# Batch statistics inside the fourth pass and a last stage in lots of four tiles

## The reference

```python
    out = D_inv[:, None] * jax.ops.segment_sum(e_feat[col], row, num_segments=num_nodes)
    out = out + b
    mean = out.mean(axis=0)
    var = out.var(axis=0)
    out = gamma * (out - mean) * jax.lax.rsqrt(var + BN_EPS) + beta
    return jax.nn.relu(out)
    ...
    x = x + _L3_gnn_ref(h, edge_index, L3_gnn_hyperedge_weight, L3_gnn_W, L3_gnn_b, L3_gnn_gamma, L3_gnn_beta)
```

## Time and profile before

| | us |
|---|---|
| median of 3 runs (lowest to highest) | 2605.35 (2597.77 to 2607.53) |
| the profiled execution's own time | 2608.04 |
| its span, first to last instruction | 2606.2 |
| TensorE busy, share of the span | 2320.7, 89% |
| VectorE busy | 1603.8, 62% |
| ScalarE busy | 1230.0, 47% |
| mean granted clock of TensorE | 0.952 |

### The profile page before, as it was taken

One profiled execution on the slowest core, in us unless ns is written; L12 is line 12 of the kernel. 1 busy time (PEld: TensorE's weight loads), 2 busy tenths in 40 slices (PEclk: granted clock), 3 DMA queues, 4 the chain that ended last, 5 costly groups with the idle time before them and its releaser, 6 DMA issues. The chain is left out here.

```text
span 2606.2 us, 71305 instructions
## 1 busy us (share of the span) xinstructions
PE 2320.7 (89%) x27901; PEld 1993.0 (76%) x27901; DVE 1603.8 (62%) x3678; ACT 1230.0 (47%) x2680; POOL 44.6 (2%) x51
## 2 busy tenths in 40 slices
PE   2489999999989998999929999899998999999996
PEld 1368778878777887887828888788887888888884
DVE  6689999999999998999962333334433112121224
ACT  2478878878777786877731222222232000011113
POOL 3300000000000000000000000000000000000000
PEclk8589999999999998999969999999998999999996
DMA  6479999999999999999989999899998999999994
GB/s 191 106 157 201 216 214 208 210 218 209 212 181 220 212 212 175 222 199 212 218 211 251 283 285 283 223 260 258 258 259 208 290 288 290 263 246 248 266 270 110
DMA packets 1608879, 589.27 MB, mean 226 GB/s; under 512 B 964326, under 2 KB 1605354, under 8 KB 1608471
## 3 DMA queue, kind: packets, MB, share of 16 engines
q1 hardware_dynamic: 1604773, 579.88, 99.9%
q0 software_dynamic: 1600, 4.92, 0.7%
q10 hardware_dynamic: 2226, 0.62, 0.2%
HBM read 255.26 MB, written 89.20 MB: 132 GB/s over the span
## 5 line engine op out<-in xcount | busy, mean ns | idle before, releaser
L1174 ACT CAST stage<-ps 128x784 f16<-128x784 f32 x784 | 655.4, 836 | 106.0 <-DMA counts_by_source<-stage 69.7
L649 PE MATMUL ps<-Ha,a_tiles 128*128 128x258 f16 x4802 | 548.5, 274 | 46.6 <-ACT Ha L1221 39.2
L649 PEld LDWEIGHTS ps<-Ha,a_tiles 128*128 128x128 f16 x4802 | 470.1, 98 | 117.1 <-ACT Ha L1221 39.3
L602 PE MATMUL ps<-hot_c,hot_r 128*128 128x98 f16 x3136 | 509.5, 212 | 13.6 <-DVE hot_c L885 7.4
L603 PE MATMUL ps<-hot_c,hot_r 128*128 128x98 f16 x3136 | 503.5, 211 | 0.0
L604 PE MATMUL ps<-hot_c,hot_r 128*128 128x98 f16 x3136 | 501.7, 210 | 0.0
L1159 ACT CAST stage<-ps 128x392 f16<-128x392 f32 x784 | 397.9, 508 | 142.5 <-PE ps L585 142.5
L577 PE MATMUL ps<-g_in,wt 128*128 128x128 f16 x2401 | 431.0, 222 | 35.9 <-DVE X L897 17.3
L578 PE MATMUL ps<-g_in,wt 128*128 128x128 f16 x2401 | 429.3, 222 | 0.0
L579 PE MATMUL ps<-g_in,wt 128*128 128x128 f16 x2401 | 429.2, 222 | 0.0
L897 DVE SCALAR_TENSOR_TENSOR X<-ps,X 128x512 f32<-128x512 f32 (+1 forms) x637 | 392.4, 650 | 49.4 <-PE ps L579 49.3
(11 more groups left out here) (194 smaller groups left out, 2062.1 us busy)
## 6 DMA issues: line engine op xcount, KB each, us to landing
a_tiles<-counts_by_source SPq DMA_DIRECT2D x147, 1600.0 KB, 8.8
counts_by_source<-stage SPq DMA_DIRECT2D x49, 1600.0 KB, 8.0
gated_parts<-G SPq DMA_DIRECT2D x7, 448.0 KB, 3.6
g_in<-gated_parts SPq DMA_DIRECT2D x98, 32.0 KB, 3.1
out_x<-X SPq DMA_DIRECT2D x6, 512.0 KB
edge_table<-tab SPq DMA_DIRECT2D x1, 2448.0 KB, 10.5
wt<-stage SPq DMA_TRANSPOSE x98, 10.9
dst_run<-in_dst SPq DMA_DIRECT2D x1, 612.4 KB
```

Source lines behind the costliest of these rows:

```text
L602: mm(into(0), rows_, codes(0), start=v == 0, stop=True, skip_group_check=True)
L649: last = mm(ps[:, c % 2, 0:PARTS], a_slot(ph, c, i), moving[:, i], start=i == 0, stop=i == TILES - 1)
L1174: a.copy(stage[:, b, 0:2, 0:TILES, u * SET_COLS:(u + 1) * SET_COLS], of).then_inc(s("hi_done"), 1)
```

## The change

- In pass four, in odd steps from j = 5, VectorE takes the statistics of a pair of tiles of `OT` (256 columns), behind its sum of tile j. It waits for the block of tile j-4 (`upd_done4` at j-3). In the loop, `OT` and `stats` are addressed by a register. Behind the branch two statistics are left (columns 5888 to 6144 and 6144 to 6250), and 25 are joined in place of 13.
- The last stage goes in 13 lots of four tiles (`lot_tiles`; the last lot has one tile), all as written-out code. ScalarE normalises 512 columns in one instruction into one of three buffers of `ybig`, which lies where `hbig` of pass one was. TensorE turns four blocks into one bank, with banks 4 to 7 in turn, and signals once. VectorE adds 512 columns in one instruction.
- SyncE sends each lot on its own: twelve transfers of 256 KB and the one of 53 KB.

```diff
+def lot_tiles(n):
+
+    return slice(4 * n, min(4 * n + 4, TILES))
...
+        ybig, _ = at("ybig", [P, 3, 4, P], F32, o2 - 2 * SET * P * 4)
...
-            for g in range(6):
-                sp.wait_ge(s("x_out"), 8 * (g + 1))
-                sp.dma_start(out[g * 8 * P:(g + 1) * 8 * P].rearrange("(i p) f -> p i f", p=P), X[:, g * 8:(g + 1) * 8, :]).then_inc(s("out_stored"), 16)
-            sp.wait_ge(s("x_out"), TILES)
+            for n in range(FOURS - 1):
+                sp.wait_ge(s("x_out"), n + 1)
+                sp.dma_start(out[n * 4 * P:(n + 1) * 4 * P].rearrange("(i p) f -> p i f", p=P), X[:, lot_tiles(n), :]).then_inc(s("out_stored"), 16)
+            sp.wait_ge(s("x_out"), FOURS)
...
-                if on(j):
-                    pe.wait_ge(s("y_ready"), j + 1)
-                    if later(j, 2):
-                        pe.wait_ge(s("x_out"), j - 1)
-                    tr(ps[:, 4 + c % 2, 0:P], hrow[:, c % SLOTS], ident[:]).then_inc(s("y_turned"), 1)
+            for n in range(FOURS):
+                pe.wait_ge(s("y_ready"), n + 1)
+                if n >= 4:
+                    pe.wait_ge(s("x_out"), n - 3)
+                tiles = lot_tiles(n)
+                for i in range(tiles.stop - tiles.start):
+                    last = tr(ps[:, 4 + n % 4, i * P:(i + 1) * P], ybig[:, n % 3, i], ident[:])
+                last.then_inc(s("y_turned"), 1)
...
+                        if ph == 4 and c % 2 and later(j, 5):
+                            n = k * (SLOTS // 2) + (c - 5) // 2
+                            dve.wait_ge(s("upd_done4"), j - 3)
+                            pair = OT[:, 2 * n:2 * n + 2] if isinstance(n, int) else OT[:, bass.ds(n * 2, 2)]
+                            v.bn_stats(row(stats, n), pair.rearrange("p i n -> p (i n)"))
...
-            lots = [(a, min(a + 512, NODES)) for a in range(0, NODES, 512)]
-            for n, (a, z) in enumerate(lots):
-                last = v.bn_stats(stats[:, n], flat[:, a:z])
+            for n in (GROUPS - 2, GROUPS - 1):
+                last = v.bn_stats(stats[:, n], flat[:, 2 * n * P:min(2 * (n + 1) * P, NODES)])
...
-            c2(v.bn_aggr(fin[:, 0:2], stats[:, 0:len(lots)].rearrange("p n s -> p (n s)")))
+            c2(v.bn_aggr(fin[:, 0:2], stats[:, 0:GROUPS].rearrange("p n s -> p (n s)")))
...
-                if on(j):
-                    dve.wait_ge(s("y_turned"), j + 1)
-                    v.tensor_tensor(row(X, j), row(X, j), ps[:, 4 + c % 2, 0:P], ALU.add).then_inc(s("x_out"), 1)
+            for n in range(FOURS):
+                dve.wait_ge(s("y_turned"), n + 1)
+                tiles = lot_tiles(n)
+                xs = X[:, tiles].rearrange("p i f -> p (i f)")
+                v.tensor_tensor(xs, xs, ps[:, 4 + n % 4, 0:(tiles.stop - tiles.start) * P], ALU.add).then_inc(s("x_out"), 1)
...
-                if on(j):
-                    if later(j, SLOTS):
-                        act.wait_ge(s("y_turned"), j - (SLOTS - 1))
-                    a.activation(hrow[:, c % SLOTS], row(OT, j), ACT.Relu, bias=fin[:, 7:8], scale=fin[:, 5:6]).then_inc(s("y_ready"), 1)
+            for n in range(FOURS):
+                if n >= 3:
+                    act.wait_ge(s("y_turned"), n - 2)
+                tiles = lot_tiles(n)
+                y = ybig[:, n % 3, 0:tiles.stop - tiles.start].rearrange("p i n -> p (i n)")
+                a.activation(y, OT[:, tiles].rearrange("p i n -> p (i n)"), ACT.Relu, bias=fin[:, 7:8], scale=fin[:, 5:6]).then_inc(s("y_ready"), 1)
```

More of the change, by code:

```diff
@@ L448, in _ @@
             branch(sp, layers)
-            for g in range(6):
-                sp.wait_ge(s("x_out"), 8 * (g + 1))
-                sp.dma_start(out[g * 8 * P:(g + 1) * 8 * P].rearrange("(i p) f -> p i f", p=P), X[:, g * 8:(g + 1) * 8, :]).then_inc(s("out_stored"), 16)
-            sp.wait_ge(s("x_out"), TILES)
+            for n in range(FOURS - 1):
+                sp.wait_ge(s("x_out"), n + 1)
+                sp.dma_start(out[n * 4 * P:(n + 1) * 4 * P].rearrange("(i p) f -> p i f", p=P), X[:, lot_tiles(n), :]).then_inc(s("out_stored"), 16)
+            sp.wait_ge(s("x_out"), FOURS)
             sp.dma_start(out[(TILES - 1) * P:NODES], X[0:LAST, TILES - 1, :]).then_inc(s("out_stored"), 16)
-            sp.wait_ge(s("out_stored"), 16 * 7)
+            sp.wait_ge(s("out_stored"), 16 * FOURS)
         @block.gpsimd
@@ L683, in _ @@
             branch(pe, layers)
-            def last_step(j, k, c):
-                if on(j):
-                    pe.wait_ge(s("y_ready"), j + 1)
-                    if later(j, 2):
-                        pe.wait_ge(s("x_out"), j - 1)
-                    tr(ps[:, 4 + c % 2, 0:P], hrow[:, c % SLOTS], ident[:]).then_inc(s("y_turned"), 1)
-            tiles_loop(pe, last_step, 0)
+            for n in range(FOURS):
[6 more added lines that the diff above has]
+                last.then_inc(s("y_turned"), 1)
         @block.vector
@@ L1099, in _ @@
             v.tensor_tensor(fin[:, 7:8], cols[:, 3:4], fin[:, 6:7], ALU.subtract).then_inc(s("batch"), 1)
-            def last_step(j, k, c):
-                if on(j):
-                    dve.wait_ge(s("y_turned"), j + 1)
-                    v.tensor_tensor(row(X, j), row(X, j), ps[:, 4 + c % 2, 0:P], ALU.add).then_inc(s("x_out"), 1)
-            tiles_loop(dve, last_step, 0)
+            for n in range(FOURS):
[3 more added lines that the diff above has]
+                v.tensor_tensor(xs, xs, ps[:, 4 + n % 4, 0:(tiles.stop - tiles.start) * P], ALU.add).then_inc(s("x_out"), 1)
         @block.scalar
@@ L1263, in _ @@
             act.wait_ge(s("batch"), 1)
-            def last_step(j, k, c):
-                if on(j):
-                    if later(j, SLOTS):
-                        act.wait_ge(s("y_turned"), j - (SLOTS - 1))
-                    a.activation(hrow[:, c % SLOTS], row(OT, j), ACT.Relu, bias=fin[:, 7:8], scale=fin[:, 5:6]).then_inc(s("y_ready"), 1)
-            tiles_loop(act, last_step, 0)
+            for n in range(FOURS):
[4 more added lines that the diff above has]
+                a.activation(y, OT[:, tiles].rearrange("p i n -> p (i n)"), ACT.Relu, bias=fin[:, 7:8], scale=fin[:, 5:6]).then_inc(s("y_ready"), 1)
 _INS = ["x", "src", "dst", "edge_weight", "L0_gnn_W", "L0_gnn_W_gate", "L0_gnn_b_gate", "L1_gnn_W", "L1_gnn_b",
```

## The result

The changed kernel takes 2590.25 us (median of 7 runs, 2584.78 to 2594.58), beside 2606.26 for the one before (7 runs, 2597.77 to 2610.79). The ratio is 0.9933, 95% interval 0.9918 to 0.9948: faster by 0.7%, which is 17 us (the two medians lie 16.0 us apart). The forecast was 19.6 us less, 2585.7.

What follows compares the result with a forecast made beforehand. TensorE bounds nearly all the kernel, relay latency its end. Gains of 6.1 us ahead of the relay and 13.5 in it make 19.6, off the 2605.35 median: 2585.7 us, range 2578 to 2597.5.

Steps and rivals of the forecast that it cites:

- VectorE's restart: Behind the branch: 2.71 us before statistics start, possibly counted from VectorE's last operation, now a pair's statistic; +0.35 us.
- statistics at the end: Behind the fourth pass: 13 statistics of 7.39 us become two of 0.58 us together, a gain of 6.8 us.
- pause ahead of the aggregate: Between the last statistic and the aggregate on VectorE: the prediction gave no added wait here, 0 us.
- aggregate: Joining the statistics at the end: it reads 150 numbers in place of 78, a loss of 0.33 us (0 to 0.5).
- relay, first activation to the end: Last stage, ScalarE to TensorE to VectorE to output: lots of four replace single tiles, 13.5 us less.
- fourth pass: Pair statistics there were costed at nothing: VectorE is idle 4.8 us per tile, a pair's statistic takes about 0.41.
- Part 2: The last stage in 13 lots with four banks and three buffers: latency replaced by bandwidth, 13.5 us less.
- four paces: Last stage, per lot: ScalarE 0.73 us, TensorE 0.86, VectorE 0.68, transfer 0.904; the slowest, the transfer, sets the pace.
- The 2.37 us behind the last large burst: End of the span: the last 53 KB transfer stays as it is, 2.37 us, mostly at 44 GB/s.
- rival C: Behind the branch: code loading comes out of cover and delays ScalarE or TensorE, losing 1 to 2.7 us; 14%.
- TensorE's clock: Last stage: clock stays at 0.50, 1.2 GHz, so four transposes take 0.86 us per lot.
- the 2 that the prediction named: Sign of being right, at the end: the adds finish some 2 us ahead of the last bytes.

Runs made afterwards that it cites:

- half_stored: The changed kernel storing only two of the four tiles of each lot; 21.07 us from VectorE's last sum to the end, against 23.99.
- four_banks: The kernel before with four PSUM banks in turn in place of two, still one tile per instruction; ratio 0.9975 to the kernel before.
- lots_only: The changed kernel with all 13 statistics back at the end and none in the fourth pass, lots kept; ratio 0.9944 to the kernel before.
- pairs_thrice: The changed kernel taking each pair's statistics three times in the fourth pass; 22.37 us from VectorE's last sum to the end, against 23.99.
- pad_split: The changed kernel with 64 never-run VectorE instructions shifting the code and the last transfer sent as 96 and 10 rows; ratio 0.9918 to the kernel before.

## Why the prediction was right, and where it was not

The direction, the size (17 us by the ratio, 18.3 in the end part, against 19.6) and the mechanism of both parts hold. One wait was missed. Term by term, in us:

| term | predicted | measured |
|---|---|---|
| VectorE's restart | +0.35 | -0.03 (2.71 to 2.68) |
| statistics at the end | -6.81 | -6.79 (7.39 to 0.60) |
| pause ahead of the aggregate | 0 | +1.72 (0.04 to 1.76) |
| aggregate | +0.33 | +0.32 (0.51 to 0.83) |
| relay, first activation to the end | -13.5 | -13.5 (30.4 to 16.9) |
| fourth pass | 0 | +0.5 (last sum at 2564.41, not 2563.91), within the spread |
| sum, change of the span | -19.6 | -17.8 (2606.2 to 2588.4) |

- **Part 2 came out to a tenth of a microsecond.** Measured, with the forecast in brackets: activations 0.81 (0.80), adds 0.69 (0.68), a lot every 0.85 (0.86) for the first six, first lot done 2.71 us after its activation starts (2.79), 11 us of output without a pause (10.85). The step that carried it was to compare four paces and take the transfer; half_stored shows that it is the bound, four_banks that latency was it before. The 2.37 us behind the last large burst should have been 2.34 by the prediction's own figures (2606.2 - 2603.86), which changes nothing.
- **The step that failed is the way from the branch to the aggregate.** I counted one wait for code, the 2.71 us, and put its danger on the other engines: rival C had ScalarE late because the long statistics no longer cover it. ScalarE wasn't late: its root starts 0.04 us behind VectorE's operation ahead of it. (C's reckoning was off too: 2.71 us from the end of ScalarE's last operation, 2565.54, is 2568.25 and not 2567.9, still in time.) VectorE itself waited a second time, 1.76 us ahead of the aggregate, which the prediction had at nothing. That these lie in C's 1 to 2.7 is luck, since engine and reason were others. What the view could have told: in the earlier trace rows code packets still arrive after VectorE's restart at 2566.62, though nothing in the trace says whose they are.
- **The restart** was sized by the wrong rule. The 1.07 us behind OT didn't follow pair 22. Eleven of the twelve kernels that leave the branch first restart 2.64 to 2.85 us after the sum, with no statistic behind it (lots_only 2.85, four_banks 2.64), one (2.68) or three (pairs_thrice 2.76), and pad_split at 3.03. So the delay doesn't wait for VectorE's queued work to end; at what point it starts stays open.
- **TensorE's clock** was assumed to stay at 1.2 GHz. It rose to 2.4 GHz at 2578.4, after 6.0 us in which the transposes left no gap; in the relay before, busy for 13.9 of 19 us, it had stayed low. From then on the adds came every 0.60 us. The sum didn't need it, since the output was the bound at either clock: the adds ended at 2582.5, and the last bytes of the lots left at about 2586.3, 3.8 us behind and not the 2 that the prediction named.
- The remaining half microsecond lies ahead of the last sum, whose place differs by up to 28 us between the profiles. Its cause was not looked for; as TensorE's idle time in the fourth pass is 13.0 us with three times the statistics and 12.8 and 13.4 with none, nothing lays it to the change.

## What to carry to other kernels

When a serial stretch shows every engine idle in turn, write down the pace of each engine and of the transfer for one lot: the largest is the time you can reach, and more banks get you part of it even without larger lots. An edit also moves all the code behind it, and with it the places where an engine waits for code: behind a jump, allow for a pause that neither kernel's data explains (1.8 us here, a tenth of the whole gain). To tell a wait for code from a wait for data, add work behind the suspected place and see where the pause stays, then shift the code with instructions that never run.

## What the runs showed of the hardware beyond that

- A transfer's issue on SyncE takes 0.37 us while the DMA engines have room (all twelve of half_stored, 0.37 to 0.39) and up to 0.87 for 256 KB when they are full (changed kernel); behind bursts of 512 KB the last one took 1.81 us. These are about the times of one such burst at 290 GB/s (0.90 and 1.81), which points at the issue being held until a transfer ahead is done. Whether other work on the issuing engine would be held as well, no run here tried.
- A transfer of 106 rows runs at 42 to 44 GB/s, as the earlier trace rows show, and one of 96 rows beside one of 10 is done 0.8 us sooner. How many of the 16 engines take part was not seen by itself.
